# A vision tower with soft-routed experts on one core: residual by an identity matmul, the values' transfers one unit later, and two parts' logits and dispatch moved forward

## What is computed

```python
h = patches(x) @ W_proj + b_proj + pos_emb              # 16 x 36 tokens, 192 wide
h = h + attention(layernorm(h))                         # 12 heads of 16, softmax over 36 tokens
z = layernorm(h)
xn = rms_norm(z) * norm_weight
logits = l2_normalize(slots) * scale @ l2_normalize(xn) # 64 slots x 36 tokens an image
dispatch, combine = softmax(logits, over tokens), softmax(logits, over slots)
y = dispatch @ xn                                       # one row for each slot and image
y = gelu(y @ fc1[slot] + b1) @ fc2[slot] + b2           # 64 experts, 192 -> 768 -> 192
h = h + y combined by combine
```

## Time and profile before

| | |
|---|---|
| median of three runs | 221.08 us |
| profiled execution | 221.91 us |
| its span | 220.2 us |
| PE busy | 196.4 us, 89% of the span |
| DVE, ACT, POOL busy | 63.9, 64.3, 45.3 us |
| transfers | 80.68 MB, 366 GB/s over the span |
| chain that ended last | PE 48%, DMA 41%, DVE 4% |
| mean granted TensorE clock | 0.974 of full speed |

### The profile page before, as it was taken

One profiled execution on the slowest core, in us unless ns is written; L12 is line 12 of the kernel. 1 busy time (PEld: TensorE's weight loads), 2 busy tenths in 40 slices (PEclk: granted clock), 3 DMA queues, 4 the chain that ended last, 5 costly groups with the idle time before them and its releaser, 6 DMA issues.

```text
span 220.2 us, 4816 instructions
## 1 busy us (share of the span) xinstructions
PE 196.4 (89%) x2048; PEld 129.7 (59%) x2048; DVE 63.9 (29%) x153; ACT 64.3 (29%) x161; POOL 45.3 (21%) x91
## 2 busy tenths in 40 slices
PE   6899999999999998999999999767896779768964
PEld 6899876566767656556465655443464336514642
DVE  1556563589874531121011211100110011000113
ACT  2553433346464354050322304101210121002200
POOL 7701068585472310101001010100010000000000
PEclk9999999999997999999999999969999999979998
DMA  6999949999999999999999999999999999999912
GB/s 166 277 237 417 390 126 356 310 329 390 419 410 414 410 366 397 387 428 422 411 411 423 425 407 411 419 426 411 413 427 414 416 412 409 424 419 409 391 51 80
DMA packets 17827, 80.68 MB, mean 366 GB/s; under 512 B 2697, under 2 KB 4398, under 8 KB 13774
## 3 DMA queue, kind: packets, MB, share of 16 engines
q1 hardware_dynamic: 17806, 80.38, 94.6%
HBM read 79.46 MB, written 0.91 MB: 365 GB/s over the span
## 4 chain that ended last, share of the span: by engine, by line
PE 48%; DMA 41%; DVE 4%; issue 2%; ACT 2%; POOL 1%; DVEq 0%; POOLq 0%; ACTq 0%
DMA ring<-in_L_ffn_fc_weight_dram 41%; PE ps L1285 9%; PE ps L1312 7%; PE ps L917 6%; PE ps L984 4%; PE ps L911 3%; PE ps L1259 3%; PE ps L1137 2%; PE ps L1028 2%; PE ps L1002 2%; PE ps L942 2%; PE ps L1248 2%; PE ps L1298 1%; PE ps L1016 1%; PE ps L1041 1%
## 5 line engine op out<-in xcount | busy, mean ns | idle before, releaser
L1285 PE MATMUL ps<-ring,qkvT 128*32 128x384 f32 x384 | 42.2, 581 | 10.3 <-DMA ring<-in_L_ffn_fc_weight_dram 9.9
L1312 PE MATMUL ps<-ring,x_space 128*32 128x192 f32 x768 | 36.2, 339 | 6.2 <-DMA ring<-in_L_ffn_fc_weight_dram 5.4
L1312 PEld LDWEIGHTS ps<-ring,x_space 128*32 128x32 f32 x768 | 24.4, 113 | 17.2 <-DMA ring<-in_L_ffn_fc_weight_dram 7.7
L888 DVE TENSOR_TENSOR region_p<-ps,b1T 128x384 f32<-128x384 f32 x16 | 8.8, 557 | 80.6 <-PE ps L1298 80.6
L1285 PEld LDWEIGHTS ps<-ring,qkvT 128*32 128x32 f32 x384 | 12.6, 113 | 31.6 <-issue 26.4
L646 ACT ACTIVATE x_space<-ps,row_scale 128x384 f32<-128x384 f32 x16 | 15.1, 944 | 45.3 <-PE ps L1285 45.3
L911 PEld LDWEIGHTS ps<-ident 128*128 128x128 f32 x116 | 16.6, 224 | 6.4 <-issue 4.6
L911 PE MATMUL ps<-ident 128*128 128x128 f32 x116 | 18.7, 319 | 1.8 <-POOL neg_half L384 1.8
L1259 PE MATMUL ps<-projT,soft_space 128*108 128x192 f32 (+1 forms) x96 | 19.1, 329 | 0.4 <-ACT projT L683 0.4
L683 ACT COPY projT<-ps 128x192 f32<-128x192 f32 x8 | 2.6, 320 | 56.3 <-PE ps L1312 56.3
L469 POOL COPY bias_space<-ident 64x128 f32<-64x128 f32 x8 | 2.2, 286 | 81.5 <-PE ps L1248 81.5
(11 more groups left out here) (139 smaller groups left out, 220.3 us busy)
## 6 DMA issues: line engine op xcount, KB each, us to landing
ring<-in_L_ffn_fc_weight_dram SPq DMA_DIRECT2D x31, 2304.0 KB, 22.4
ring<-in_L_ffn_fc_weight_dram SPq DMA_DIRECT2D x3, 768.0 KB, 7.3
ring<-in_x_dram SPq DMA_DIRECT2D x2, 864.0 KB, 8.2
ring<-in_L_tok_W_proj_dram SPq DMA_DIRECT2D x1, 576.0 KB, 7.4
ring<-in_L_attn_w_qkv_dram SPq DMA_DIRECT2D x1, 432.0 KB, 10.6
out_dram<-h SPq DMA_DIRECT2D x2, 162.0 KB
value_store<-ring SPq DMA_DIRECT2D x1, 258.2 KB
ring<-value_store SPq DMA_DIRECT2D x3, 86.1 KB
```

What stands on the lines that cost most here:

```text
L888: dve.tensor_tensor(pre[:, pr, :, :].rearrange("p c (k b) -> p c k b", b=B), ps[:, 2 + pr, 0:384].rearrange("p (c k b) -> p c k b", c=3, b=B),
L1285: mm = pe.matmul(ps[32 * k:32 * k + 32, pr, 0:FF // 2], y_group[:, g % 2, j, 2 * pr + qq, :], w[:, qq, j, :, 3 * hf:3 * hf + 3], start=(j ...
L1312: mm = pe.matmul(ps[32 * q:32 * q + 32, 4, 0:D], gact[:, q // 2, k, 32 * l:32 * l + 32], w[:, q, c, :], start=(l == 0 and c == 0), stop=(l ...
```

## The change

It has five parts, in one diff.

1. **Residual by identity matmul.** `attn_tile` no longer adds `h`. Instead PE opens each tile's accumulation with identity times `h` (`open_projection`) and adds the projection on top; DVE takes statistics and centres straight from PSUM, and ACT copies the sum from PSUM into `h` later (`keep_h`). The semaphore `h2_ready` becomes `h_kept`, and the tiles' PSUM banks are dealt out anew.
2. **Values' transfers one unit back.** The first store stands before unit 3 and not unit 2, the first loads and other stores before unit 4, the second loads before unit 5.
3. **Order.** `turn_tok(0)`, `token_logits(0)`, `turn_logits(0)`, the logits of part 1 and the dispatch of part 1 stand earlier in PE's list; `turn_logits(2)` stands behind `slot_inputs(1)`. ACT's and DVE's lists follow.
4. **No dummies there.** Both `keep_busy(7, 2)` are gone.
5. **POOL.** Two steps of `norms` share one wait.

```diff
-        PROJECTED = (2, 2, 2, 4, 5, 4)
+        PROJECTED = (2, 2, 4, 5, 0, 6)
...
-        LOGITS = (2, 0, 2)
-        DISPATCH = (1, 6, 7)
-        SLOT_IN = (4, 5, 0, 4, 5, 5)
+        LOGITS = (2, 7, 2)
+        DISPATCH = (1, 1, 7)
+        SLOT_IN = (4, 5, 3, 4, 5, 5)
...
-                if n == 2:
+                if n == 3:
                     store_values(0, 3)
-                elif n == 3:
+                elif n == EARLY:
                     sp.wait_ge(v_blank, 2)
                     sp.wait_ge(v_stored[0], 16)
                     load_values(0, 0, 3 * TPI)
                     store_values(3, 5)
                     store_values(5, TT)
-                elif n == EARLY:
+                    sp.wait_ge(embedded, TT)
+                elif n == EARLY + 1:
                     sp.wait_ge(v_stored[1], 32)
                     load_values(1, 3 * TPI, B)
-                    sp.wait_ge(embedded, TT)
...
+            def keep_h(t):
+
+                act.wait_ge(attn_done, t + 1)
+                act.wait_ge(centered, t + 1)
+                act.copy(h[0:rows(t), t, :], ps[0:rows(t), PROJECTED[t], 0:D]).then_inc(h_kept, 1)
...
                 if i in (5, 6):
                     square(i - 5)
+                    keep_h(i - 5)
             exp_probs(PAIRS - 1)
             keep_probsT(PAIRS - 2)
             keep_probsT(PAIRS - 1)
             keep_oT(PAIRS - 3)
+            keep_tokT(0)
             keep_oT(PAIRS - 2)
             keep_oT(PAIRS - 1)
+            scale_logits(0)
             square(2)
-            keep_tokT(0)
             square(3)
-            scale_logits(0)
+            keep_tokT(1)
+            keep_h(2)
             square(4)
-            keep_tokT(1)
+            scale_logits(1)
             square(5)
             keep_tokT(2)
             exp_dispatch(0)
-            scale_logits(1)
+            keep_h(3)
+            exp_dispatch(1)
             scale_logits(2)
-            exp_dispatch(1)
             exp_dispatch(2)
+            keep_h(4)
+            keep_h(5)
...
-                dve.tensor_tensor(h[0:r, t, :], ps[0:r, PROJECTED[t], 0:D], h[0:r, t, :], ALU.add).then_inc(h2_ready, 1)
-                dve.wait_ge(h2_ready, t + 1)
-                step(dve.bn_stats(stats[0:r, t, :], h[0:r, t, :]))
+                step(dve.bn_stats(stats[0:r, t, :], ps[0:r, PROJECTED[t], 0:D]))
...
             shift_dispatch(0)
+            shift_dispatch(1)
             diag_dispatch(0)
-            shift_dispatch(1)
+            diag_dispatch(1)
             shift_dispatch(2)
-            diag_dispatch(1)
             diag_dispatch(2)
...
+            def open_projection(t):
+
+                r = rows(t)
+                if t == 0:
+                    pe.wait_ge(k_ready, 4)
+                elif t == 1:
+                    pe.wait_ge(h_kept, 1)
+                elif t < 4:
+                    pe.wait_ge(shifted, 5 + t)
+                elif t == 4:
+                    pe.wait_ge(probsT_ready, PAIRS - 1)
+                else:
+                    pe.wait_ge(oT_ready, 2 * PAIRS - 2)
+                pe.matmul(ps[0:r, PROJECTED[t], 0:D], ident[0:r, 0:r], h[0:r, t, :], start=True, stop=False)
...
                     for t in PROJECTED_AT.get(i, ()):
+                        open_projection(t)
                         project_output(t)
+            turn_tok(0)
             turn_probs(PAIRS - 2)
+            open_projection(2)
             project_output(2)
             turn_probs(PAIRS - 1)
             turn_output(PAIRS - 3)
             probs_times_values(PAIRS - 2)
+            open_projection(3)
             probs_times_values(PAIRS - 1)
             project_output(3)
+            token_logits(0)
             turn_output(PAIRS - 2)
+            open_projection(4)
             turn_output(PAIRS - 1)
-            turn_tok(0)
+            open_projection(5)
             project_output(4)
             project_output(5)
-            token_logits(0)
+            turn_logits(0)
             turn_tok(1)
-            turn_logits(0)
-            keep_busy(7, 2)
+            token_logits(1)
             turn_tok(2)
-            token_logits(1)
+            turn_logits(1)
             token_logits(2)
             turn_dispatch(0)
-            turn_logits(1)
-            turn_logits(2)
-            keep_busy(7, 2)
             slot_inputs(0)
             turn_dispatch(1)
+            slot_inputs(1)
+            turn_logits(2)
+            slot_inputs(2)
             turn_dispatch(2)
-            slot_inputs(1)
-            slot_inputs(2)
             slot_inputs(3)
```

More of the change, by code:

```diff
@@ L209, in vit_tower_kernel @@
         centered = sem("centered")
-        attn_done, h2_ready, moments2 = sem("attn_done"), sem("h2_ready"), sem("moments2")
+        attn_done, h_kept, moments2 = sem("attn_done"), sem("h_kept"), sem("moments2")
         scale2_ready, sq_ready, rnorm_ready = sem("scale2_ready"), sem("sq_ready"), sem("rnorm_ready")
@@ L446, in norms @@
                     pool.wait_ge(sq_ready, t + 1)
-                    step(pool.tensor_scalar(ssq[:, t:t + 1], ssq[:, t:t + 1], floor[:, t:t + 1], None, ALU.max))
+                    pool.tensor_scalar(ssq[:, t:t + 1], ssq[:, t:t + 1], floor[:, t:t + 1], None,
+                                       ALU.max).then_inc(pool_step, 1)
+                steps[0] += 2
+                pool.wait_ge(pool_step, steps[0])
                 pool.tensor_tensor(rnorm[:, a:b], ssq[:, a:b], neg_half[:, a:b],
@@ L765, in center @@
                 dve.wait_ge(moments2, t + 1)
-                dve.scalar_tensor_tensor(out=xn[0:r, t, :], in0=h[0:r, t, :], scalar=mv[0:r, t, 0:1],
+                dve.scalar_tensor_tensor(out=xn[0:r, t, :], in0=ps[0:r, PROJECTED[t], 0:D], scalar=mv[0:r, t, 0:1],
                                          in1=norm_row[0:r, :], op0=ALU.subtract, op1=ALU.mult).then_inc(centered, 1)
@@ L1051, in turn_output @@
                 mm.then_inc(o_turned, 1)
+            def open_projection(t):
[11 more added lines that the diff above has]
+                pe.matmul(ps[0:r, PROJECTED[t], 0:D], ident[0:r, 0:r], h[0:r, t, :], start=True, stop=False)
             def project_output(t):
                 r = rows(t)
+                if t == 0:
+                    pe.wait_ge(ab_in, 16)
                 pe.wait_ge(oT_ready, 2 * (last_pair(t) + 1))
[L1057 to L1065, removed]
                 for c in range(2):
@@ L1068, in project_output @@
                     mm = pe.matmul(ps[0:r, PROJECTED[t], 0:D], oT[0:k, c, t * TR:t * TR + r], projT[0:k, c, :],
-                                   start=(c == 0), stop=(c == 1))
+                                   start=False, stop=(c == 1))
                 mm.then_inc(attn_done, 1)
@@ L1090, in token_logits @@
                 if part == 0:
-                    pe.wait_ge(h2_ready, 3)
+                    pe.wait_ge(h_kept, 2)
                 elif part == 1:
-                    pe.wait_ge(probsT_ready, PAIRS - 1)
+                    pe.wait_ge(oT_ready, 2 * PAIRS)
                 else:
@@ L1116, in turn_dispatch @@
                     pe.wait_ge(probsT_ready, PAIRS)
+                elif part == 1:
+                    pe.wait_ge(ddiag_ready, 2)
                 else:
-                    pe.wait_ge(oT_ready, 2 * PAIRS)
+                    pe.wait_ge(d_shifted, 2)
                 for n, t in enumerate((2 * part, 2 * part + 1)):
@@ L1128, in slot_inputs @@
                 pe.wait_ge(ddiag_ready, t + 1)
-                if t == 0:
-                    pe.wait_ge(h2_ready, TT)
-                elif t >= 3:
+                if t < 2:
+                    pe.wait_ge(h_kept, 3 + t)
+                elif t == 2:
+                    pe.wait_ge(tokT_ready, PARTS)
+                else:
                     pe.wait_ge(y_kept, (1, 2, 2)[t - 3])
@@ L1270, in first_layer @@
                     if g == 0:
+                        pe.wait_ge(h_kept, TT)
                         pe.wait_ge(first_direct, 2)
```

## The result

The changed kernel takes 228.97 us (median of four runs, 227.34 to 230.72) against 221.1 us before (220.76 to 224.04 in four): the ratio is 1.0346, 95% interval 1.030 to 1.039. It is slower, as forecast, but by 7.9 us and not by 3.8. The profiled execution took 228.31 us, its span 226.6.

The account below looks back on a forecast made before the run. The expert layer's start, set by PE's own list, was taken to bound the time: +2.2 - 1.1 + 2.7 - 0.4 + 0.4 = +3.8 us on 221.08 gives 224.9 us, own range 224.0 to 226.0, 8 in 10 within 222.8 to 226.8.

Parts of the forecast that it names:

- The bound: Time moves with the later of two limits: weight bytes behind the hole, and PE's way to the expert layer.
- The hole at 28 us: Gap of 3.1 us in the weight stream; filling it gains nothing unless the expert layer starts earlier too.
- both limits: Bytes behind the hole at 28 us and PE's way to the expert layer, said to coincide at 74.91 us.
- 2.2 - 1.1 + 2.7: PE's terms: six identity matmuls +2.2 us, dummies removed -1.1, new waits less the old order's +2.7.
- five waits: New PE waits on ACT or DVE, from open_projection(1) to slot_inputs(2); with 0.1 for a copy, 3.4 us.
- The dummies: Removing both keep_busy pairs on PE saves 0.45 us for the first and 0.6 for the second, together -1.1 us.
- The wait for the values: PE waits at its first product with the loaded values: 0.4 us, bounds 0 and 2.8.
- The clock: PE's stretch at 1.2 GHz before the layer keeps its length but partly lies over waits: -0.4 us.
- the replay: Engines' lists replayed from 46 us with the timeline's durations; 75.0 us for the observed 74.91, low clock costing 1.3.
- (b) to (e): PE waits before the logits of parts 1 and 2, slot_inputs(0) and slot_inputs(2): 0.65, 0.35, 0.6, 1.1 us.
- Rival 1: Longer waits: clock low for two stretches or values hold PE 1.5 us or more; 226.0 to 227.5 us, chance 0.17.
- the 0.8 us: Amount by which the median of the kernel before lay below its profiled execution, carried over to the forecast.

Follow-up runs that it names:

- e1: Kernel before with only the values' transfers one unit later; 222.93 us, ratio 1.004.
- e7: Changed kernel with nine dummy matmuls in PE's waits and the values' transfers where they were before; 224.51 us, ratio 1.0103.
- e4: Changed kernel with nine dummy matmuls placed where PE waits; 224.69 us, ratio 1.0174.
- e2: Kernel before without the two pairs of dummy matmuls; 222.94 us, ratio 1.0055.
- e8: The changed kernel run once more, nothing altered; 230.45 us.
- e12: Changed kernel, no dummies, with the values' transfers where they were before; 229.17 us, ratio 1.0319.
- e6: Changed kernel with dummies in PE's waits and the residual added by DVE again; 223.65 us, ratio 1.007.
- e10: Changed kernel with nine dummy matmuls in PE's waits, run again in another set; 229.07 us, ratio 1.023.

## Why the prediction was right or wrong

**The bound: right in the main.** The time goes with the start of the expert layer. From that start to the end of the span it is 145.3 us before, 145.5 in the changed kernel, and 145.2 to 146.1 in nine other profiles whose layer starts between 73.72 and 81.87 us; the three whose layer began at 1.2 GHz have 146.8 to 147.5. The hole at 28 us was filled and given back before unit 9, as the sum said, and putting it back cost nothing: 145.2 us with the late values and 145.3 with the old place, both with dummies. That both limits coincided at 74.91 us is not borne out. Without the two pairs of dummies, and with the hole as before, the layer starts 0.6 us earlier and the span is 0.7 us shorter, so the hole did not hold the end back there. With the hole filled (`e1`) the layer starts 1.2 us earlier and the span is only 0.5 us shorter; why is open.

**What does not hang on the clock: right in sum, 3.8 us.** Three profiles with the clock up all the way to the layer show it, counted from PE's first product with the values: 30.19 us in the old order (`e1`), 34.02 and 33.91 in the new order with dummies in its waits (`e7`, `e4`), so +3.8 and +3.7 us for the forecast 2.2 - 1.1 + 2.7. All five waits are in their places, 2.9 us for 3.3. Two parts were off in opposite directions. The dummies were not worth 1.1 us: `e2` has the layer 0.6 us earlier and no shorter time, and the first pair cost nothing, because the copy of the earlier trace rows ends at 64.80 us, so that the transposes could not start near 64.6. And the identity matmuls stand partly in waits for ACT, 0.83 us in two places, that the forecast did not have. That the total fits so well is partly luck. DVE's adds were not priced by themselves; statistics from PSUM take 0.37 us, those from SBUF took 0.36.

**The wait for the values: right in kind, too small.** I took 0.4 us between 0 and 2.8. Seven profiles with the late transfers show 0.37, 0.85, 0.91, 0.92, 1.00, 1.87 and 1.99 us at that place, two more start that product 0.3 and 0.4 us after the 43.26 of the earlier trace rows without a bracket, and five with the old place have no wait. The row had told only that the loads were in time, not by how much, and I chose near the lower end without a row for it. The working was loose as well: 2.6 MB from 30.2 us, at 183 GB/s to 32 us and 413 later, put the loads' turn at 37.4 us and not near 38.5. It is the windows behind, with 240 and 364 GB/s up to 36 us, that lead to 38.5 to 39. The first loads are issued 3.2 us later, and the store that they wait for is the small transfer behind a big one; the trace agrees with the ring order that the Trainium skill states in "DMA: Bandwidth & Descriptors", section "Queues, rings and completion order".

**The clock: the step that failed.** "The new order has more and longer waits at that place and no dummies; I expect a stretch of the same length", at -0.4 us against before. It was 10.2 us long. From the first product with the values to the layer the changed kernel takes 37.01 us, against 33.91 and 34.02 at the full clock: a price of 3.0 to 3.1 us. Two other profiles of that order without dummies (`e8`, `e12`) pay 2.6 us before the layer and, where the low clock reaches into it, another 1.5 to 2.1 us behind. By the same rows the stretch of the kernel before costs 31.65 - 30.19 = 1.5 us (1.3 in the replay). So the term is +1.6 us and not -0.4. With it the sum is 3.8 + 1.6 + 0.85 = 6.2 us, and 6.2 were measured at the layer's start.

The two terms on one line of the text, more waits and the same clock, did not go together. Four profiles of the changed order with (b) to (e) open have 10.2 to 13.7 us at 1.2 GHz. Four with (b) to (e) filled with dummies have 0, 0, 0 and 6.8 us; a fifth (`e6`) has none there, but 10.2 us earlier, behind its wait for the values. Two with the longest wait taken away and four dummies have 3.4. Rival 1 named the right mechanism, but with twice the length as its worst, and its 226.0 to 227.5 us ended below the median.

**From the profile to the median.** The profiled run is the second shortest of four. The three others differ from it by -1.0, +1.3 and +2.4 us at mean granted clocks of 0.961, 0.948 and 0.948, and it has 0.955. That the length of the stretch varies from run to run is likely, not shown: there is a trace of one of these runs only, and two with the same mean clock lie 1.1 us apart. I had carried over the 0.8 us by which the median of before lay under its profile; here the median lies 0.7 us over it. That is 1.5 us of the 4.1 by which the forecast was short; the clock's term is 2.0, the values' 0.45, and the rest is below 0.2.

What stays open: why the dummies held the clock at that place in four profiles and not in a fifth (`e10`; it began with the longest wait for the values, which may have shifted all that follows), whether it is the idle time they fill or the work they add that counts, and how much of the 1.6 us each single wait carries.

## What to carry to other kernels

When a transfer stream is released by an engine, find the later of the two limits first, and price a filled hole at nothing until the releasing engine is earlier too. An engine that is nearly saturated by its own in-order list gets slower by the instructions given to it, however idle its neighbours are, unless they fall into its waits (six openings of 2.5 us and a wait of 0.5 cost 1.8 here), and by every pair of neighbours in its list in which the second needs the first to come back through another engine. On TensorE such waits were paid twice here, once as idle time (2.9 us) and once as the clock of the work around them (3.0 to 3.1 us): a reordering that opens several of them close together should also be priced with a low clock over the whole place.

## What was not expected of the hardware

- One program's time spreads by 3 us in 221 and more from run to run, and the granted clock explains a part of it: the same kernel had no stretch at 1.2 GHz on its way to the layer in one profile (`e4`) and 6.8 us of it in another (`e10`). Only a part: the kernel before had 220.77 us at a mean clock of 0.969 and 223.21 us at 0.977.
- Dummies in PE's waits cost next to nothing at the full clock (0.89 us from `turn_dispatch(0)` to `slot_inputs(0)` with them in `e7`, 0.83 without in `e12`). At the low clock they outlast the wait: eight instructions took 1.16 us at 2.4 GHz and 2.08 us at 1.2 GHz, and 2.52 us from `turn_logits(2)` to `slot_inputs(2)` (`e10`) where it was 1.64 without them (`e12`).
